# One wait per batch instead of two before the row gathers of a two-layer graph attention kernel

## The chip, the cores and the metric

The kernel runs on one core of one Trainium2 chip. A core has five engines that run side by side: TensorE (PE: matmuls, with its weight loads shown as PEld), VectorE (DVE), ScalarE (ACT), GpSimd (POOL) and SyncE (SP), and 16 DMA engines that move data. The engines have queues of their own and meet only at semaphores: an instruction counts a semaphore up when it is done, and another engine waits until the count is high enough. The metric is the device time of one execution in microseconds (us). The time before is 1787.6 us, the median of three executions (1787.34, 1787.60 and 1789.18 us).

## The reference

Two layers of graph attention over 3125 nodes with 128 features and 53125 directed edges, sorted by their destination. For each edge the keys and values of its source node are needed; softmax runs over the edges of one destination. Cut to what matters here:

```python
# layer 0 (x is normalised first); layer 1 adds an edge term to k and v
q, k, v = h @ Wq + bq, h @ Wk + bk, h @ Wv + bv
e = sum(q[d_all] * k[s_all], axis=-1) / sqrt(16)      # 8 heads of 16
p = exp(e - segment_max(e, d_all)[d_all])
alpha = p / segment_sum(p, d_all)[d_all]
agg = segment_sum(alpha[:, :, None] * v[s_all], d_all)
x = residual + agg.reshape(n, 128) @ Wo + bo
x = x + gelu(layer_norm(x) @ W1 + bf1) @ W2 + bf2
# layer 1: k_j = k[src] + edge_attr @ We, v_j = v[src] + edge_attr @ We, then the same
```

## The kernel before

**Tiles.** The edges are padded to 53248 and cut into 26 batches (`G`) of 16 tiles (`J`) of 128 edges, one edge to a partition. Each layer first computes the keys and values of all nodes and stores them in a table in HBM (`kv_table`, 256 floats a node). Then it goes once through the 26 batches. After that come the output projection, the normalisation and the feed-forward part, blocks of 128 nodes at a time.

**A batch.** GpSimd fetches the rows of its 2048 source nodes with 16 indirect DMAs (L464), one for each tile of 128 edges, into one of four slots of the tile `KV` (`SLOTS` = 4, slot = n % 4). The first eight count the semaphore `gathered[s][0]` up, the last eight `gathered[s][1]`. VectorE waits for the one before it works on the tiles of the first half (`add_edges`, L996), and for the other before those of the second half. TensorE makes each edge's query row from one-hot matrices (L732, L733), VectorE multiplies it with the keys (L1008) and adds up the heads (L1015), and the softmax of the batch before runs in between. VectorE then weighs the values in place in `KV` (`weigh`, L1120), and TensorE adds them up by destination in four quarters of four tiles (`add_up`, L778). Each quarter counts `agg_ready` up by one, so a batch adds 4. After the second quarter the first half of the slot is free, after the fourth the whole slot.

**What sets the order around the change.** Each engine's program is written out in Python, in rounds: in round n VectorE does the logits of batch n and the softmax of n - 1, TensorE adds up batch n - 2, and GpSimd runs freely ahead as far as the four slots allow. GpSimd has nothing else to do during the batches. Its `gather(n)` waits for the list of indices (`idx_loaded`), and before each half for `agg_ready` of batch n - 4: for the count after its second quarter before the first eight gathers, for the count after its fourth before the last eight. `pool.sem_inc(S["pool_go"], 1)` is an instruction for that wait to sit on; nobody reads the semaphore. SyncE loads the indices of batch n + 4 when the second half of batch n has landed (`indices`, L299).

Of the kernel before, what the change touches and what calls it, by code (L numbers as in the profile page):

```python
# [26 lines left out]
J = 16  # L27
G = 26
# [9 lines left out]
SLOTS = 4  # L38
# [3 lines left out]
def build(nc, a, out):  # L42
# [4 lines left out]
    kv_table = nc.dram_tensor("kv_table", (NP, 2 * D), F32, kind="Internal").ap()  # L47
# [6 lines left out]
    with ExitStack() as ctx:  # L54
# [3 lines left out]
        def sem(name):  # L58
# [6 lines left out]
        KV = sb("KV", [P, SLOTS, J, 2 * D])  # L65
# [11 lines left out]
        idx = sb("idx", [P, SLOTS, J], U32)  # L77
# [95 lines left out]
        S = {n: sem(n) for n in """x_loaded x2_loaded dst_loaded dste_loaded gates_in first_weights weights_loaded  # L173
            rel_stored block_loaded gate_stored edges_stored edges_loaded
            rel_loaded gate_loaded windows_stored last_loaded out_stored""".split()}
# [47 lines left out]
        def done(name, n):  # L223


            return S[name], n + START
# [18 lines left out]
        gathered = [[sem(f"gathered{s}{hh}") for hh in range(2)] for s in range(SLOTS)]  # L245
# [151 lines left out]
        @block.gpsimd  # L397
        def _(pool):
            g = nc.gpsimd
            g.memset(We[:, :], 0.0).then_inc(S["we_zeroed"], 1)  # L400
            g.memset(ones[:, :], 1.0).then_inc(S["consts_made"], 1)
            g.memset(ones3[:, :], 1.0).then_inc(S["consts_made"], 1)
            g.memset(one_col[:, :], 1.0).then_inc(S["consts_made"], 1)
            g.memset(ident[:, :], 0.0).then_inc(S["consts_made"], 1)
            g.memset(hsel[:, :], 1.0).then_inc(S["consts_made"], 1)
            g.memset(max_row[:, :], 0.0).then_inc(S["consts_made"], 1)
            g.memset(sum_rows[:, :], 0.0).then_inc(S["consts_made"], 1)
            g.memset(SUG[:, :], 0.0).then_inc(S["consts_made"], 1)
            g.memset(QT[:, NP:NP + P], 0.0).then_inc(S["consts_made"], 1)
            g.memset(minus_big[:, :], -BIG).then_inc(S["consts_made"], 1)  # L410
            pool.wait_ge(*done("consts_made", 10))
            g.affine_select(out=ident[:, :], in_=ident[:, :], compare_op=ALU.not_equal, fill=1.0,
                            base=0, pattern=[[-1, P]], channel_multiplier=1).then_inc(S["consts_made"], 1)
            by_head = hsel[:, :].rearrange("p (h c) -> p h c", h=H)
            g.affine_select(out=by_head, in_=by_head, compare_op=ALU.is_ge, fill=0.0,
                            base=0, pattern=[[-C, H], [0, C]], channel_multiplier=1).then_inc(S["consts_made"], 1)
            g.iota(iota_row[:, :], pattern=[[1, P]], base=0, channel_multiplier=0,
                   allow_small_or_imprecise_dtypes=True).then_inc(S["consts_made"], 1)
            g.iota(minus_part[:, :], pattern=[[-P, 2]], base=0, channel_multiplier=-1,
                   allow_small_or_imprecise_dtypes=True).then_inc(S["consts_made"], 1)  # L420
            g.iota(iota_part[:, :], pattern=[[P, 2]], base=0, channel_multiplier=1,
                   allow_small_or_imprecise_dtypes=True).then_inc(S["consts_made"], 1)
            pool.wait_ge(*done("consts_made", 12))
            g.affine_select(out=by_head, in_=by_head, compare_op=ALU.is_ge, fill=0.0,
                            base=C - 1, pattern=[[C, H], [0, C]], channel_multiplier=-1).then_inc(S["consts_made"], 1)

            g.memset(own_tiles, 1.0).then_inc(S["gates_made"], 1)
            g.memset(SAME[:, CH:CH + 4], 0).then_inc(S["gates_made"], 1)
            by_tile = own_tiles.rearrange("p (q k) -> p q k", k=TK)
            pool.wait_ge(*done("gates_made", 1))  # L430
            g.affine_select(out=by_tile, in_=by_tile, compare_op=ALU.is_equal, fill=0.0,
                            base=0, pattern=[[-1, TP], [0, TK]], channel_multiplier=1).then_inc(S["gates_made"], 1)
            g.memset(AGG[:, :], 0.0).then_inc(S["gates_made"], 1)

            pool.wait_ge(S["weights_loaded"], 16 * WEIGHTS)
            g.tensor_tensor(FB[:, 1, :], FB[:, 1, :], GB[:, 1, :], ALU.add).then_inc(S["fb_made"], 1)
            for l in range(2):
                if l:

                    def keep(n, k):  # L440
                        pool.wait_ge(*done("xn_ready", n + (2 * NB + 1)))
                        pool.sem_inc(S["pool_go"], 1)
                        g.tensor_copy(X[:, ds(n * P, P)], xn[k]).then_inc(S["x_kept"], 1)

                    def shift(n, k):
                        pool.wait_ge(*done("batch_step", n + 1))
                        pool.sem_inc(S["pool_go"], 1)
                        g.tensor_tensor(X[:, ds(n * P, P)], X[:, ds(n * P, P)], GB[:, 3, :], ALU.add).then_inc(S["x_shifted"], 1)

                    pipelined(pool, (keep, 4), (shift, 0))  # L450

                for k in range(4):
                    pool.wait_ge(kv_stored[k], 16 * kv_uses[k] * (l + 1))

                def gather(n):
                    s, u = n % SLOTS, n // SLOTS + 1 + uses[n % SLOTS] * l
                    pool.wait_ge(idx_loaded[s], u * 16)
                    if l == 0 and n == 2:
                        pool.wait_ge(S["edges_stored"], 64)
                    for hh in range(2):  # L460
                        pool.wait_ge(*done("agg_ready", n * 4 + (4 * G * l + 2 * hh + 2 - 4 * SLOTS)))
                        pool.sem_inc(S["pool_go"], 1)
                        for j in range(hh * 8, hh * 8 + 8):
                            g.indirect_dma_start(KV[:, s, j, :], None, kv_table,  # L464
                                                 bass.IndirectOffsetOnAxis(ap=idx[:, s, j:j + 1], axis=0)).then_inc(gathered[s][hh], 16)

                for n in range(G):
                    gather(n)

                if l == 0:  # L470

                    for b, w in quads:
                        at = slice(b * P, (b + w) * P)
                        pool.wait_ge(*done("res_ready", b + w))
                        pool.sem_inc(S["pool_go"], 1)
                        g.tensor_tensor(X[:, at], X[:, at], Y[:, at], ALU.add).then_inc(S["x_pair"], w)
                        pool.wait_ge(*done("x_pair", b + w))
                        pool.sem_inc(S["pool_go"], 1)
                        x3 = X[:, at].rearrange("p (b d) -> p b d", b=w)
                        g.tensor_tensor(x3, x3, FB[:, 0, :].unsqueeze(1).broadcast_to([P, w, D]), ALU.add).then_inc(S["x_summed"], w)  # L480
                else:
                    pool.wait_ge(*done("fb_made", 1))

                    def affine(n, k):
                        at = ds(n * P, P)
                        pool.wait_ge(*done("xn_ready", n + (3 * NB + 1)))
                        pool.sem_inc(S["pool_go"], 1)
                        g.tensor_tensor(Y[:, at], Y[:, at], GB[:, 0, :], ALU.mult).then_inc(S["ln_affine"], 1)
                        pool.wait_ge(*done("ln_affine", n * 3 + 1))
                        pool.wait_ge(*done("tp_ready", n + (3 * NB - 1)))  # L490
                        pool.sem_inc(S["pool_go"], 1)
                        g.tensor_tensor(hN[k], Y[:, at], GB[:, 1, :], ALU.add).then_inc(S["ln_affine"], 1)
                        pool.wait_ge(*done("ln_affine", n * 3 + 2))
                        pool.sem_inc(S["pool_go"], 1)
                        g.tensor_tensor(Y[:, at], Y[:, at], FB[:, 1, :], ALU.add).then_inc(S["ln_affine"], 1)

                    blocks(pool, affine)


                    def scale_last(n, k):  # L500
                        pool.wait_ge(*done("xn_ready", n + (4 * NB + 1)))
                        pool.wait_ge(*done("x_out", n - 1))
                        g.tensor_tensor(hN[k], xn[k], GB[:, 2, :], ALU.mult).then_inc(S["ln_last"], 1)

                    blocks(pool, scale_last)
# [871 lines left out]
```

## Time and profile before

| | us |
|---|---|
| median of three executions | 1787.6 |
| lowest and highest | 1787.34, 1789.18 |
| profiled execution, from its first to its last instruction (the span) | 1423.2 |
| what the median has beyond that span | 364.4 |
| GpSimd busy in the span | 901.0 (63%), of it the 832 gathers 810.3 |
| VectorE busy | 1076.5 (76%) |
| TensorE busy | 1072.8 (75%) |
| ScalarE busy | 840.3 (59%) |

The profile gives no time of the profiled execution other than its span, so the span is set beside the median of the executions that were timed. The 364.4 us between them lie before the first and after the last instruction that the trace holds, or in the way in which the two are taken; no view divides them. Times inside the span are read as microseconds from its start. "Idle before" is the time in which an engine stood before an instruction, and the name behind it is the work whose end released it; "issue" means that the engine waited for nothing that the profile shows. Register and semaphore instructions are not counted as busy, and no view has rows of their own for them.

### The profile page before, as it was taken

The numbers are of one execution on the slowest core, as the hardware profiler recorded it, in microseconds if no ns is written. First come the engines' busy times: TensorE is split into PE (matmuls) and PEld (weight loads), VectorE is DVE, ScalarE is ACT, GpSimd is POOL, SyncE is SP. The second block draws the span as 40 slices with busy tenths as digits, with TensorE's granted clock in tenths as the row PEclk, the third lists the DMA queues.
The fourth block names the chain that finished last, engine by engine and source line by source line (L and its number), as shares of the span: only waits on it lengthen the run. The fifth ranks groups of instructions, "written<-read, shape, count | busy, mean of one in ns | idle before, by whom it ended". The sixth has DMA issues, their size and how long they took to land. (4 is left out here: it accounts for less than half of the span.)

```text
span 1423.2 us, 28503 instructions
## 1 busy us (share of the span) xinstructions
PE 1072.8 (75%) x6809; PEld 956.7 (67%) x6809; DVE 1076.5 (76%) x2695; ACT 840.3 (59%) x2605; POOL 901.0 (63%) x1028
## 2 busy tenths in 40 slices
PE   3937678767877787768896788888888888887790
PEld 1436677667866776758735677787787778776690
DVE  5538877787877787865443888988988898897557
ACT  1615776676667666644443467766776676576351
POOL 2177777777777777531046777777777777770453
PEclk9967877787777777778897989999999999898795
DMA  5385555555555565420024567667766766671001
GB/s 157 106 182 178 173 188 194 191 155 189 193 186 159 192 193 171 137 91 0 7 79 141 176 211 223 197 193 220 214 199 196 224 207 189 219 229 48 1 1 45
DMA packets 100659, 222.50 MB, mean 156 GB/s; under 512 B 34875, under 2 KB 49882, under 8 KB 96941
## 3 DMA queue, kind: packets, MB, share of 16 engines
q0 software_dynamic: 39936, 109.11, 26.8%
q1 hardware_dynamic: 57927, 109.78, 22.8%
q10 hardware_dynamic: 2662, 2.05, 0.5%
q8 instruction: 56, 0.92, 0.3%
q14 instruction: 78, 0.64, 0.1%
HBM read 184.86 MB, written 36.00 MB: 155 GB/s over the span
## 5 line engine op out<-in xcount | busy, mean ns | idle before, releaser
L464 POOL DMA_INDIRECT KV<-kv_table,idx x832 | 810.3, 974 | 301.5 <-issue 247.4
L732 PE MATMUL PS<-QT,OHT 128*128 x1664 | 401.6, 330 | 146.5 <-DVE OHT L990 122.3
L732 PEld LDWEIGHTS PS<-QT,OHT 128*128 128x128 f32 x1664 | 317.9, 236 | 166.1 <-issue 164.6
L733 PE MATMUL PS<-QT,OHT 128*128 x1664 | 390.4, 324 | 0.0
L733 PEld LDWEIGHTS PS<-QT,OHT 128*128 128x128 f32 x1664 | 319.1, 238 | 0.0
L592 ACT ACTIVATE AGG<-AGG,PC,RCS x800 | 309.3, 387 | 3.1 <-ACT AGG L588 2.4
L1008 DVE TENSOR_TENSOR PR<-KV,PS 128x512 f32<-128x512 f32 x208 | 140.6, 676 | 105.6 <-DMA KV<-kv_table,idx 103.7
L778 PE MATMUL PS<-OH,KV 128*128 128x128 f32 x1600 | 208.4, 280 | 2.9 <-DVE OH L1110 1.2
L588 ACT ACTIVATE AGG<-PS 128x127 f32 x800 | 208.0, 260 | 1.0 <-issue 0.7
L778 PEld LDWEIGHTS PS<-OH,KV 128*128 128x128 f32 x1600 | 196.7, 197 | 5.6 <-issue 2.6
L584 ACT ACTIVATE PC<-PS 128x4 f32<-128x4 f32 x200 | 33.5, 168 | 267.1 <-PE PS L778 256.0
L1001 DVE TENSOR_TENSOR KV<-KV,PS 128x1024 f32<-128x1024 f32 x104 | 125.3, 1205 | 76.0 <-PE PS L743 47.5
L1015 DVE TENSOR_REDUCE Ls<-PR 128x32 f32<-128x512 f32 x208 | 139.7, 672 | 0.2
L1120 DVE TENSOR_TENSOR KV<-KV,PS 128x512 f32<-128x512 f32 x208 | 128.6, 680 | 0.4 <-PE PS L753 0.3
L568 ACT ACTIVATE OHT<-REL,minus_part 128x1024 f32<-128x1024 bf16 x104 | 113.0, 1134 | 19.9 <-PE PS L733 19.9
L743 PE MATMUL PS<-We,EA 128*128 128x256 f32 x416 | 118.3, 424 | 0.0
L571 ACT ACTIVATE OHT<-OHT,one_col 128x1024 f32<-128x1024 f32 x104 | 112.9, 1133 | 0.0
L753 PE MATMUL PS<-ident,AL 128*128 128x128 f32 x52 | 21.1, 405 | 105.9 <-DVE AL L1095 105.9
L743 PEld LDWEIGHTS PS<-We,EA 128*128 128x128 f32 x416 | 86.9, 226 | 10.6
L753 PEld LDWEIGHTS PS<-ident,AL 128*128 128x128 f32 x52 | 8.4, 161 | 118.5 <-DVE AL L1095 118.5
L660 ACT ACTIVATE KV<-PS,bf 128x128 f32<-128x128 f32 x208 | 59.4, 368 | 44.5 <-PE PS L854 37.3
L990 DVE TENSOR_SCALAR OHT<-REL,iota_part 128x1024 f32<-128x1024 bf16 x104 | 79.5, 766 | 0.0
(158 smaller groups left out, 1352.2 us busy)
## 6 DMA issues: line engine op xcount, KB each, us to landing
REL<-rel_dram SPq DMA_DIRECT2D x52, 512.0 KB, 4.4
window_dram<-OH SPq DMA_DIRECT2D x25, 1024.0 KB
OH<-window_dram SPq DMA_DIRECT2D x50, 512.0 KB, 6.1
KV<-kv_table,idx POOLq DMA_INDIRECT x832
EA<-in_edge_batch SPq DMA_DIRECT2D x52, 256.0 KB
kv_table<-KV SPq DMA_DIRECT2D x52, 128.0 KB, 1.7
X<-in_x SPq DMA_DIRECT2D x2, 832.0 KB, 10.1
GATES<-edge_gates SPq DMA_DIRECT2D x8, 208.0 KB, 10.0
```

The source lines that it names most:

```text
L464: g.indirect_dma_start(KV[:, s, j, :], None, kv_table, bass.IndirectOffsetOnAxis(ap=idx[:, s, j:j + 1], axis=0)).then_inc(gathered[s][hh], 16)
L568: sc.activation(OHT[:, 1, nf, :], REL[:, 8 * P:16 * P], ACT.Abs, bias=minus_part[:, nf:nf + 1]).then_inc(S["oht2_step"], 1)
L588: sc.activation(AGG[:, ds(at + 1, P - 1)], bank[:, m, 1:P], ACT.Copy).then_inc(S["act_col"], 1)
L592: sc.activation(AGG[:, ds(at, 1)], AGG[:, ds(at, 1)], ACT.Identity, bias=PC[:, m:m + 1], scale=RCS[:, n % SLOTS, j:j + 1]).then_inc(S["act ...
L732: te.matmul(o, OHT[:, q // 2, 0, e0:e0 + P], QT[:, ds(blk, P)], start=True, stop=False)
L733: last = te.matmul(o, OHT[:, q // 2, 1, e0:e0 + P], QT[:, ds(blk + P, P)], start=False, stop=True)
L743: last = te.matmul(PS[2 + q % 2][:, 2 * m * D:2 * (m + 1) * D], EA[:, e0:e0 + P], We[:, :], start=True, stop=True)
L778: last = te.matmul(PS[4 + q % 2][:, m * P:(m + 1) * P], KV[:, n % SLOTS, j, D:2 * D], at[:, j * P:(j + 1) * P], start=True, stop=True)
L1001: v.tensor_tensor(kv, kv, ep, ALU.add).then_inc(S["e_used"], 1)
L1008: v.tensor_tensor(PR[:, q % 2, :].rearrange("p (j d) -> p j d", j=4), KV[:, n % SLOTS, 4 * q:4 * q + 4, 0:D], PS[q % 2][:, :].rearrange("p ...
L1015: v.tensor_reduce(Ls[:, :].rearrange("p (h j) -> p j h", h=H)[:, 4 * q:4 * q + 4, :], PR[:, q % 2, :].rearrange("p (j h c) -> p j h c", j= ...
L1120: v.tensor_tensor(v4, v4, at, ALU.mult).then_inc(S["pv_ready"], 1)
```

## The change

In `gather(n)` the loop over the two halves is gone. GpSimd waits once per batch, for the count of `agg_ready` that stood before the second half, and then issues all 16 gathers. The semaphore that each gather counts up is the same as before.

```diff
-                    for hh in range(2):
-                        pool.wait_ge(*done("agg_ready", n * 4 + (4 * G * l + 2 * hh + 2 - 4 * SLOTS)))
-                        pool.sem_inc(S["pool_go"], 1)
-                        for j in range(hh * 8, hh * 8 + 8):
-                            g.indirect_dma_start(KV[:, s, j, :], None, kv_table,
-                                                 bass.IndirectOffsetOnAxis(ap=idx[:, s, j:j + 1], axis=0)).then_inc(gathered[s][hh], 16)
+                    pool.wait_ge(*done("agg_ready", n * 4 + (4 * G * l + 4 - 4 * SLOTS)))
+                    pool.sem_inc(S["pool_go"], 1)
+                    for j in range(J):
+                        g.indirect_dma_start(KV[:, s, j, :], None, kv_table,
+                                             bass.IndirectOffsetOnAxis(ap=idx[:, s, j:j + 1], axis=0)).then_inc(gathered[s][j // 8], 16)
```

GpSimd's queue at batches 4 and 5 of the first layer, before the change. A row is one instruction or a run of like ones; `idx_loaded0` is the list of indices of slot 0, `agg_ready` the count of added-up quarters.

```order
L464 DMA KV<-kv_table,idx 128x256 [waits idx_loaded0,agg_ready]
L464 DMA KV<-kv_table,idx 128x256 x7
L464 DMA KV<-kv_table,idx 128x256 [waits agg_ready]
L464 DMA KV<-kv_table,idx 128x256 x7
L464 DMA KV<-kv_table,idx 128x256 [waits idx_loaded1,agg_ready]
L464 DMA KV<-kv_table,idx 128x256 x7
L464 DMA KV<-kv_table,idx 128x256 [waits agg_ready]
```

The same place of GpSimd's queue after the change, with the first gather of batch 6 as its last row.

```order
L463 DMA KV<-kv_table,idx 128x256 [waits idx_loaded0,agg_ready]
L463 DMA KV<-kv_table,idx 128x256 x15
L463 DMA KV<-kv_table,idx 128x256 [waits idx_loaded1,agg_ready]
L463 DMA KV<-kv_table,idx 128x256 x15
L463 DMA KV<-kv_table,idx 128x256 [waits idx_loaded2,agg_ready]
```

The wait between the eighth and the ninth gather is gone from each of the 52 batches; its count is now waited for eight gathers earlier. No gather has changed its place.

GpSimd's queue at the end of the first layer's batches before the change; `res_ready` counts blocks of the output projection.

```order
L464 DMA KV<-kv_table,idx 128x256 [waits idx_loaded1,agg_ready]
L464 DMA KV<-kv_table,idx 128x256 x7
L464 DMA KV<-kv_table,idx 128x256 [waits agg_ready]
L464 DMA KV<-kv_table,idx 128x256 x7
L476 TENSOR_TENSOR X<-X,Y 128x512 [waits res_ready]
L480 TENSOR_TENSOR X<-X,FB 128x512 [waits x_pair]
```

The same place after the change, from the last gathers of batch 24 on.

```order
L463 DMA KV<-kv_table,idx 128x256 x15
L463 DMA KV<-kv_table,idx 128x256 [waits idx_loaded1,agg_ready]
L463 DMA KV<-kv_table,idx 128x256 x15
L475 TENSOR_TENSOR X<-X,Y 128x512 [waits res_ready]
L479 TENSOR_TENSOR X<-X,FB 128x512 [waits x_pair]
```

What follows the gathers stands where it stood. The instructions of the other four engines are the same in the same order.

## Rows read from the trace of the kernel before

**Rows 1.** Busy time by stage: layer 0 from 66 us, layer 1 from 752 us.
```profile
core 0: us, PE busy (x) PEld busy (x) DVE busy (x) ACT busy (x) POOL busy (x), PEclk, DMA share, GB/s
66.00:597.00 531.00, 392.03 (x2526) 374.07 (x2525) 406.17 (x977) 342.11 (x1055) 404.17 (x416) 0.76 0.59 181
...
752.00:1285.00 533.00, 432.20 (x2883) 397.40 (x2882) 452.26 (x978) 336.54 (x1033) 406.01 (x416) 0.90 0.66 203
```

**Rows 2.** Waits of layer 0's steady part, 147 to 597 us: total, times, longest.
```profile
POOL KV L464 <- issue: 102.4, 336, 0.3
...
DVE PR L1008 <- DMA KV<-kv_table,idx: 82.0, 22, 4.9
...
POOL KV L464 <- PE PS L778: 5.2, 17, 0.3
```

**Rows 3.** Waits of layer 1's steady part, 833 to 1284 us.
```profile
POOL KV L464 <- issue: 107.2, 352, 0.3
...
DVE KV L1001 <- PE PS L743: 44.6, 22, 3.1
...
DVE KV L1001 <- DMA KV<-kv_table,idx: 1.3, 1, 1.3
```

**Rows 4.** All gathers: duration in ns, lowest, median and highest.
```profile
L464 POOL DMA_INDIRECT KV<-kv_table,idx x832: 942/946/1472, 65.9 to 1283.6; - x167
```

**Rows 5.** Timeline, GpSimd, batch 4 of layer 0: start, duration; eighth and ninth gather, first of batch 5.
```profile
147.55 0.95 POOL L464 DMA_INDIRECT KV<-kv_table,idx  x1 [0.31 <-issue]
...
156.47 0.95 POOL L464 DMA_INDIRECT KV<-kv_table,idx  x1 [0.30 <-issue]
157.73 0.95 POOL L464 DMA_INDIRECT KV<-kv_table,idx  x1 [0.30 <-issue]
...
167.80 0.94 POOL L464 DMA_INDIRECT KV<-kv_table,idx  x1 [0.30 <-issue]
```

**Rows 6.** Timeline, TensorE: adding up batch 0 of layer 0, the first slot given back.
```profile
120.17 2.86 PE L778 MATMUL PS<-OH,KV 128*128 128x128 f32 x16
124.65 1.06 PE L778 MATMUL PS<-OH,KV 128*128 128x128 f32 x8
127.33 1.06 PE L778 MATMUL PS<-OH,KV 128*128 128x128 f32 x8
```

**Rows 7.** Timeline, TensorE and GpSimd: batch 9 added up, batch 13's first gather, layer 0.
```profile
302.75 2.06 PE L778 MATMUL PS<-OH,KV 128*128 128x128 f32 x16
306.78 1.06 PE L778 MATMUL PS<-OH,KV 128*128 128x128 f32 x8
309.46 1.06 PE L778 MATMUL PS<-OH,KV 128*128 128x128 f32 x8
...
330.77 0.95 POOL L464 DMA_INDIRECT KV<-kv_table,idx  x1 [0.30 <-issue]
```

**Rows 8.** Timeline, TensorE and GpSimd, layer 1: batch 21 added up, batch 25's first gather.
```profile
1242.47 1.95 PE L778 MATMUL PS<-OH,KV 128*128 128x128 f32 x16
1246.04 1.06 PE L778 MATMUL PS<-OH,KV 128*128 128x128 f32 x8
1249.59 1.06 PE L778 MATMUL PS<-OH,KV 128*128 128x128 f32 x8
...
1264.33 0.95 POOL L464 DMA_INDIRECT KV<-kv_table,idx  x1 [0.30 <-issue]
```

**Rows 9.** Timeline, layer 1: batch 14 added up, batch 18's first gather.
```profile
1103.66 1.06 PE L778 MATMUL PS<-OH,KV 128*128 128x128 f32 x8
...
1120.61 0.95 POOL L464 DMA_INDIRECT KV<-kv_table,idx  x1 [0.30 <-issue]
```

**Rows 10.** Timeline, layer 0: fifth gather of a half (its first at 299.87).
```profile
299.87 0.95 POOL L464 DMA_INDIRECT KV<-kv_table,idx  x1 [0.30 <-issue]
...
304.87 0.96 POOL L464 DMA_INDIRECT KV<-kv_table,idx  x1 [0.30 <-PE PS L778]
```

**Rows 11.** Timeline, GpSimd: the first gather of layer 1.
```profile
752.10 0.99 POOL L464 DMA_INDIRECT KV<-kv_table,idx  x1 [2.18 <-DMA kv_table<-KV]
```

## The prediction

> **What bounds the kernel now.** I read the busy time by stage first, then the waits of each stage, then GpSimd's timeline at the places where the two waits stand. The stages [rows 1] show that the gathers fill both passes over the batches: 416 of them in the 531 us of layer 0 and 416 in the 533 us of layer 1, together 1064 of the span's 1423.2 us. The change touches nothing outside these. The waits of the steady part of layer 0 [rows 2] show who is last there: VectorE stands 22 times for the gathered rows, 82.0 us in all, 3.7 us per batch, while GpSimd never stands longer than 0.3 us. So GpSimd's pace is the pace of layer 0. One gather has a median of 946 ns [rows 4] and 0.30 us of idle time before it, 1.25 us together; 16 of them make 20.0 us, and the batch of [rows 5] takes 167.80 - 147.55 = 20.25 us. In layer 1 it is different [rows 3]: from 833 us on VectorE stands once, 1.3 us, for gathered rows, and 22 times, 44.6 us in all, for TensorE's edge matmuls. The loop between VectorE and TensorE sets the pace there. GpSimd still shows no idle time but the 0.3 us before each gather, so it is not held by a free slot either; it simply keeps up.
>
> What matters for this change is the row that should show GpSimd waiting for a free slot. It is there, "POOL KV L464 <- PE PS L778", 5.2 us in 17 times, longest 0.3 us [rows 2]. That is 0.3 us each, exactly what every gather has before it with no wait at all. It is the ordinary gap with another name on it, and in layer 1's steady part the row is missing.
>
> **What the change removes.** Per batch it takes one wait and the instruction that carries it out of GpSimd's queue, 52 in all. Their cost can be read at the ninth gather of a batch, before which the wait stood: 156.47 to 157.73 is 1.26 us from start to start, with 0.30 us idle [rows 5], and a gather without a wait has the same 0.30 us. The rows are rounded to 0.01 us, so one removed wait gives back at most about 0.01 us, 52 of them 0.5 us. The outer bound is that the whole gap of 0.30 us went with the wait: 26 x 0.30 = 7.8 us in layer 0, where GpSimd sets the pace, and nothing in layer 1. I take 0, because the gap before a gather with a wait is that of one without. What hides the wait is the gather that runs while the wait is being worked off.
>
> **What the change adds or moves.** The wait for the whole slot now stands before the first gather of a batch, where a wait for half of it stood. Behind it are queued all 16 gathers of the batch, and for them wait VectorE (both halves) and SyncE, which loads the next indices after the second half. The question is when the whole slot is free, against when the first gather of the batch starts.
> - Layer 0, first reuse of a slot: batch 0 is added up by 127.33 + 1.06 = 128.39 us [rows 6], and batch 4 starts its gathers at 147.55 us [rows 5]. The margin is 19.2 us. With the old wait (first half free at 120.17 + 2.86 = 123.03 us) it was 24.5 us.
> - Layer 0, steady: batch 9 is done at 309.46 + 1.06 = 310.52 us, batch 13 starts at 330.77 us [rows 7], margin 20.3 us. The old one was 330.77 - 304.81 = 26.0 us.
> - Layer 1, steady: batch 14 is done at 1103.66 + 1.06 = 1104.72 us, batch 18 starts at 1120.61 us [rows 9], margin 15.9 us.
> - Layer 1, last batch: batch 21 is done at 1249.59 + 1.06 = 1250.65 us, batch 25 starts at 1264.33 us [rows 8]. The margin is 13.7 us, the smallest of the 44 batches that reuse a slot.
>
> A margin of the gather's start is not yet one of the wait, because GpSimd's sequencer, which works off the waits, reads ahead of the engine. The trace shows it: the gather at 304.87 us is the fifth of its half and has no wait of its own, yet the trace names the adding up as what released it [rows 10]. So a wait for that count was worked off there, and the nearest half that has one begins at least four gathers, 5 us, later. I can't read the full distance from a view. It doesn't decide: while the sequencer stands at a wait, the gathers that it has already handed over go on running. What must fit between the freeing of the slot and the start of the first gather is only the handing over. The nearest row for that is the first gather of layer 1, which starts 2.18 us after its last release, with an empty queue [rows 11]. 2.2 us against 13.7 us: no gather starts later. The cost lies between 0 and 0; were the cover gone, it would be that of the slow rival below. Nothing else moves: the 832 gathers, the semaphores that they count up and every other engine's program are as they were.
>
> Here the Trainium skill speaks against the change ("Advanced Engine Details and Errata", Sequencer and Instruction Queues, Engine Queue Depths): it gives GpSimd a queue 8 instructions deep. By it the sequencer would meet the new wait about 8 x 1.25 = 10 us (an estimate with that page's depth) before the gather starts, and the margin at the wait itself would shrink from 13.7 to 3.7 us in the last batch. It would still pass without standing, so the sum stays. That [rows 10] show a wait worked off in mid-half agrees with such a queue; its depth no row here shows.
>
> **The sum.** Layer 0: 0 for the removed waits, 0 for the moved one. Layer 1: 0 and 0. The span stays at 1423.2 us, and as the 364.4 us between span and median are not touched, the median stays at 1787.6 us.
>
> **The rivals.**
> - *The removed waits were paid for (faster).* If the 0.30 us before the ninth gather fell away, layer 0 would lose 7.8 us: 1779.8 us. For it speaks that VectorE really waits for these gathers, so each 0.01 us counts 26 times. Against it speaks the equal gap with and without a wait. The Trainium skill puts 50 to 100 ns on reading a semaphore from a sequencer ("Advanced Engine Details and Errata", Miscellaneous Facts, Network/Comms). By that page the removed waits would be worth up to 26 x 0.1 = 2.6 us in layer 0 (an estimate), 1785.0 us, if they weren't hidden; the rows show no such difference. Chance of this rival: 0.04.
> - *The wait for the whole slot decides (slower).* Then gathering batch n hangs on the last quarter of batch n - 4 rather than on its second. That would lengthen a loop of four batches by the time between these quarters: 128.39 - 123.03 = 5.4 us in layer 0, 1250.65 - 1244.42 = 6.2 us in layer 1. 22 batches per layer reuse a slot, which is 5.5 rounds of four: 5.5 x 5.4 + 5.5 x 6.2 = 64 us, 1851 us. It would decide from the point at which the margin falls under the 2.2 us of handing over, that is if slots came free 11.5 us later than now in layer 1's last batch, or 14 to 18 us later in the others. For it speaks only that the margin in layer 1 is the smaller one. If it held in the last batch alone, it could not cost more than 6.2 us. Chance: 0.03.
> - *The gathers meet VectorE's instructions at another phase.* A gather's duration goes up to 1472 ns against a median of 946 [rows 4]. In layer 0 this adds 404.17 - 416 x 0.946 = 10.6 us [rows 1]. Should the removed instructions shift the gathers by a few hundredths of a microsecond, that sum could become anything from nothing to double: 1777 to 1798.2 us. Against it speaks that the starts don't move, by the above. Chance: 0.03, either way.
>
> **How the numbers follow.** Forecast 0.90, faster rival 0.04, slower rival 0.03, phase 0.03. What the measurement can tell from no change is about 0.2%, 3.6 us. The forecast lies within it, the first two rivals on their own side, the third is split. That gives faster 0.05, same 0.91, slower 0.04. The executions of before spread over 1.8 us (1787.34 to 1789.18), so the range of the forecast is the median with a little more than that on either side, 1785.4 to 1790.0 us. It takes in the skill's 2.6 us nearly whole and the 0.5 us of the rounding. The three rivals, together 0.10, are left out.
>
> **What would show it right or wrong.** In the profile after, the gathers of a batch should still take 20.2 to 20.5 us and have 0.30 us idle before each, the ninth too. If the ninth shows less, the faster rival is right. The first gather of a batch should start within some tenths of a microsecond of where it did, 13 us or more after the last quarter of the slot. If idle time over 0.3 us appears before it with L778 behind it, the slower rival is right, and then VectorE's wait for gathered rows, 3.7 us per batch in layer 0, must have grown too. The total of the gathers' durations should stay near 810 us. If it is off by more than 3 us, the phase has shifted. The prediction is wrong if the median leaves 1785.4 to 1790.0 us.

## The result and the profile after

The kernel with one wait per batch takes 2070.25 us (2062.1 to 2075.23, four runs), the kernel before in the same comparison 1788.39 us (1787.34 to 1796.03). The ratio is 1.1557, 95% interval 1.1517 to 1.1597: 282 us, 15.6%, slower. The forecast was 1787.6 us. The numbers below can't be understood without one thing: these kernels have two kinds of execution, both seen on one and the same chip at different times, one in which before takes some 1427 us and one in which it takes some 1788 us, so each time is given with that of before beside it.

The profile after is of an execution of 2067.39 us with a span of 2065.4 us. Two rows of its page, GpSimd's gathers and the largest wait of ScalarE (line numbers from L464 on are one less than before), and under them the same two rows of the page before:
```profile
L463 POOL DMA_INDIRECT KV<-kv_table,idx x832 | 793.1, 953 | 909.2 <-issue 859.0
L583 ACT ACTIVATE PC<-PS 128x4 f32<-128x4 f32 x200 | 34.1, 170 | 811.1 <-remote 715.1
...
L464 POOL DMA_INDIRECT KV<-kv_table,idx x832 | 810.3, 974 | 301.5 <-issue 247.4
L584 ACT ACTIVATE PC<-PS 128x4 f32<-128x4 f32 x200 | 33.5, 168 | 267.1 <-PE PS L778 256.0
```
The waits of the whole execution after (engine, line, what ended the wait: us in total, times, longest):
```profile
POOL KV L463 <- issue: 859.0, 830, 47.4
ACT PC L583 <- remote: 715.1, 46, 17.3
DVE KV L1000 <- remote: 394.2, 24, 44.4
PE PS L731 <- DVE PR L1007: 324.0, 30, 36.0
```
The engines' own work is nearly what it was: the gathers take 793.1 us, against 810.3 before. What grew is above all idle time; TensorE's busy time grew too, from 1072.8 to 1142.9 us, at a lower granted clock (last section). GpSimd stood no longer than 0.3 us in the steady parts of before [rows 2, 3]; now its idle time before gathers is 909.2 us in the whole execution, against 301.5 before, and up to 47.4 us at once. In before's rows VectorE waits for gathered rows or TensorE's edge matmuls, a few us at a time; now it waits 24 times, 394.2 us, for something that the profile calls "remote", a release that it can't assign.

Where GpSimd stands is seen in the timeline. Batch 0's last adding-up and batch 4's first gather, layer 0, then batch 1's last quarter and batch 5's first two gathers, and in layer 1 a batch's last quarter and a first gather:
```profile
181.92 1.06 PE L777 MATMUL PS<-OH,KV 128*128 128x128 f32 x8
183.78 0.94 POOL L463 DMA_INDIRECT KV<-kv_table,idx  x1 [35.50 <-issue]
...
214.26 1.06 PE L777 MATMUL PS<-OH,KV 128*128 128x128 f32 x8
216.11 0.94 POOL L463 DMA_INDIRECT KV<-kv_table,idx  x1 [12.21 <-issue]
217.36 0.95 POOL L463 DMA_INDIRECT KV<-kv_table,idx  x1 [0.30 <-issue]
...
1606.92 1.06 PE L777 MATMUL PS<-OH,KV 128*128 128x128 f32 x8
1608.78 0.94 POOL L463 DMA_INDIRECT KV<-kv_table,idx  x1 [14.45 <-issue]
```
In each case the first gather follows the last quarter of its slot by 0.8 us (216.11 - 215.32, 183.78 - 182.98, 1608.78 - 1607.98). The trace shows the same 0.8 us at all 44 batches that reuse a slot. So the wait for the whole slot decides at every one of them, where in [rows 5 to 9] it had 13.7 to 20.3 us to spare. Within a batch the ninth gather still has 0.30 us before it. From batch 5 to batch 25 one batch takes 30.9 us in layer 0 and 34.2 us in layer 1, against 20.4 and 20.5 us in the profile of before.

### The profile page after: what moved, and what is told of

It reads as the page before. It is cut to its first block and busy times, and to the rows that moved or that the text cites. A ratio compares the mean times of both kernels' runs of the same rounds, so it can differ in the third digit from the quotient of the medians.

```text
span 2065.4 us, 28451 instructions
## 1 busy us (share of the span) xinstructions
PE 1142.9 (55%) x6809; PEld 1017.7 (49%) x6809; DVE 1078.9 (52%) x2695; ACT 842.9 (41%) x2605; POOL 884.1 (43%) x1028
## 3 DMA queue, kind: packets, MB, share of 16 engines
q0 software_dynamic: 39936, 109.11, 18.4%
## 5 line engine op out<-in xcount | busy, mean ns | idle before, releaser
L463 POOL DMA_INDIRECT KV<-kv_table,idx x832 | 793.1, 953 | 909.2 <-issue 859.0
L731 PE MATMUL PS<-QT,OHT 128*128 x1664 | 426.1, 346 | 512.1 <-DVE PR L1007 324.0
L731 PEld LDWEIGHTS PS<-QT,OHT 128*128 128x128 f32 x1664 | 343.6, 253 | 541.8 <-issue 538.4
L732 PE MATMUL PS<-QT,OHT 128*128 x1664 | 409.5, 336 | 17.4 <-issue 17.2
L583 ACT ACTIVATE PC<-PS 128x4 f32<-128x4 f32 x200 | 34.1, 170 | 811.1 <-remote 715.1
L1000 DVE TENSOR_TENSOR KV<-KV,PS 128x1024 f32<-128x1024 f32 x104 | 125.8, 1209 | 436.8 <-remote 394.2
L732 PEld LDWEIGHTS PS<-QT,OHT 128*128 128x128 f32 x1664 | 339.9, 253 | 19.0 <-issue 19.0
L777 PE MATMUL PS<-OH,KV 128*128 128x128 f32 x1600 | 248.0, 307 | 166.8 <-ACT AGG L591 136.1
L777 PEld LDWEIGHTS PS<-OH,KV 128*128 128x128 f32 x1600 | 227.6, 220 | 169.9 <-issue 166.4
L587 ACT ACTIVATE AGG<-PS 128x127 f32 x800 | 208.4, 260 | 0.8 <-issue 0.4
L742 PE MATMUL PS<-We,EA 128*128 128x256 f32 x416 | 106.4, 390 | 0.0
L872 DVE TENSOR_TENSOR_SCAN FW<-GA,PS 128x128 f32<-128x128 bf16 x52 | 21.7, 417 | 120.8 <-issue 104.9
L742 PEld LDWEIGHTS PS<-We,EA 128*128 128x128 f32 x416 | 76.3, 199 | 7.6
```

The costliest lines, as they stand in the source:

```text
L463: g.indirect_dma_start(KV[:, s, j, :], None, kv_table, bass.IndirectOffsetOnAxis(ap=idx[:, s, j:j + 1], axis=0)).then_inc(gathered[s][j // ...
L587: sc.activation(AGG[:, ds(at + 1, P - 1)], bank[:, m, 1:P], ACT.Copy).then_inc(S["act_col"], 1)
L731: te.matmul(o, OHT[:, q // 2, 0, e0:e0 + P], QT[:, ds(blk, P)], start=True, stop=False)
L732: last = te.matmul(o, OHT[:, q // 2, 1, e0:e0 + P], QT[:, ds(blk + P, P)], start=False, stop=True)
L742: last = te.matmul(PS[2 + q % 2][:, 2 * m * D:2 * (m + 1) * D], EA[:, e0:e0 + P], We[:, :], start=True, stop=True)
L777: last = te.matmul(PS[4 + q % 2][:, m * P:(m + 1) * P], KV[:, n % SLOTS, j, D:2 * D], at[:, j * P:(j + 1) * P], start=True, stop=True)
```

## Experiments

**The kernel before, the value, and the number of waits.** Three kernels, run once each; before beside them took 1429.0 us. control changes nothing. two_full keeps two waits, both for the whole slot:
```
-pool.wait_ge(*done("agg_ready", n * 4 + (4 * G * l + 2 * hh + 2 - 4 * SLOTS)))
+pool.wait_ge(*done("agg_ready", n * 4 + (4 * G * l + 4 - 4 * SLOTS)))
```
quarters has four waits of four gathers each, each for its own quarter (`for q in range(4)`, `... + q + 1 - 4 * SLOTS`).

> The kernel before, unchanged, to see the profile of an execution that takes what the timed ones take (1788 us); the profile on which the prediction rested had a span of 1423.2 us. Theory A (the slot loop): the span is about 1786 us, 2 us under the time, and GpSimd stands for more than 0.3 us before the first or the ninth gather of a batch, behind TensorE's adding up. Rival (something outside the span): the span is 1423 us again and 364 us lie outside.

> Two waits per batch as before, but both for the whole slot (the count of the fourth quarter). Theory A (it is the value that is waited for, not the number of waits): the time of the changed kernel, 2062 to 2075 us. Rival B (the instruction between the halves matters by itself, as a pause of GpSimd's queue): the time of before, 1788 us.

> Four waits per batch, each for its own quarter of the slot, four gathers behind each. Theory A (slot loop): the first four gathers may start about 1 us earlier (TensorE adds up quarters 0 and 1 in one go) and the third four some 3 us earlier than before, over a loop of four batches: 44 x 0.25 to 44 x 1 us less than before, 1744 to 1777 us. Rival B (only the number of pauses counts): two pauses fewer cost 282 us, so two more should gain something of that order, 1500 to 1650 us. Rival C (no effect below a half): 1788 us.

Measured: 1425.71, 1426.05 and 1421.02 us. Nothing tells the three apart, and the unchanged kernel is 363 us under its time in the first comparison, so none of the three met the executions that their expectations were about. Span and time differ by 1.7 us (1424.0 and 1425.71 in control), not by 364.

**The kernel after once more.** whole is the changed kernel itself, three rounds on another chip.

> The changed kernel again, against the kernel before. In the three runs so far the kernel before took 1426 to 1429 us, not 1788, and two waits for the whole slot took 1426 us: the value that is waited for did not matter there. Theory A (the whole slot costs only in executions in which TensorE's semaphore updates come late, as the trace of the 2067 us execution shows them): where before takes 1425 to 1430 us, the changed kernel takes the same, 1421 to 1430 us. Rival (taking away the ninth gather's wait instruction is what costs, whatever the state): 1660 us or more against 1427, a ratio near 1.16.

Measured: 1427.63 us (ten runs) against 1427.19 us, ratio 1.0002, 95% interval 0.9972 to 1.0033. The same code that cost 282 us costs nothing here. Its waits from 147 to 597 us, and its first gather of batch 4:
```profile
POOL KV L463 <- issue: 107.0, 351, 0.3
...
DVE PR L1007 <- DMA KV<-kv_table,idx: 85.4, 22, 5.0
```
```profile
130.88 1.06 PE L777 MATMUL PS<-OH,KV 128*128 128x128 f32 x8
...
150.91 0.95 POOL L463 DMA_INDIRECT KV<-kv_table,idx  x1 [0.31 <-issue]
```
These answer to [rows 2, 5, 6] and are the picture that the prediction drew: 19.0 us between the last quarter (131.94) and the gather, 0.31 us idle, VectorE's 82.0 us for gathered rows now 85.4.

**Make the loop bind.** The loop of slots is the circle in which a slot is gathered into, worked on, added up and so freed for the batch four later. It binds when GpSimd has to stand until a slot is free. If this loop is what costs, it must cost in the 1427 us executions too once it has only three batches in it. half3, whole3 and quarters3 are before, after and quarters with every awaited value raised by 4, one batch:
```
-n * 4 + (4 * G * l + 2 * hh + 2 - 4 * SLOTS)
+n * 4 + (4 * G * l + 2 * hh + 2 - 4 * SLOTS + 4)
```

> The two waits of each batch ask for the halves of the batch three before instead of four before, a stricter condition, so that the loop of slots has three batches in it and has to bind if it can. Loop theory (the whole-slot wait costs only where the loop slot free, gather, add up is the limit): from the rows of before, the start of a batch's gathers to the end of its adding up is four batches of 20.5 us less the margin of 13.7 to 20.3 us, so 62 to 68 us, and a wait for half a slot is let go 5.4 to 6.2 us earlier: (56 to 63) / 3 = 18.8 to 21 us per batch, no more than 0.5 us over the 20.5 us of now, so 1425 to 1450 us. Rival (a wait costs by being there or by its place in GpSimd's queue, and not by the loop): 1427 us, as before.

> One wait per batch for the whole slot of the batch three before. Loop theory: 62 to 68 us plus 0.8 us of wake-up over three batches is 21 to 23 us per batch against 20.5, over 46 batches 25 to 115 us more than before, 1450 to 1540 us, and 5.4 to 6.2 us / 3 = 1.8 to 2.1 us per batch (some 80 to 95 us) above half3 where both bind. The idle time before each batch's first gather should be in the trace. Rival (not the loop): within 5 us of half3 and of before.

> Four waits per batch, each for its own quarter of the slot of the batch three before. Loop theory: a quarter is free still one adding-up step earlier than a half, so this is the quickest of the three, at or below half3, 1420 to 1435 us. If instead the number of waits costs, it is the slowest of the three.

Measured, with before at 1419.64 us: half3 1429.66, whole3 1544.55, quarters3 1427.5 us. GpSimd's waits for the gathers, half3 first:
```profile
POOL KV L464 <- issue: 252.8, 825, 1.8
```
```profile
POOL KV L463 <- issue: 380.3, 829, 5.4
```
And two batches of whole3, the last quarter of a slot and the first gather into it:
```profile
290.83 1.06 PE L777 MATMUL PS<-OH,KV 128*128 128x128 f32 x8
292.68 0.94 POOL L463 DMA_INDIRECT KV<-kv_table,idx  x1 [1.44 <-issue]
...
312.68 1.06 PE L777 MATMUL PS<-OH,KV 128*128 128x128 f32 x8
314.54 0.94 POOL L463 DMA_INDIRECT KV<-kv_table,idx  x1 [1.45 <-issue]
```
Again 0.8 us from the last quarter to the gather. A batch takes 23.2 us in layer 0 and 23.0 in layer 1, in half3 20.5 and 20.6. So with three batches in the loop, waiting for the whole slot costs 115 us more than waiting for halves. half3 itself doesn't bind. Within each layer the first and ninth gathers of its batches have their 0.3 us of idle time and no more, but for one with 1.8 us, though the semaphore events of GpSimd show its sequencer standing 8 to 11 us at the first wait of each batch from the fourth of a layer on. Its 10 us over before lie within the 22 us over which before spread in the comparison with whole (1418.75 to 1440.57). whole3 came out 5 us above the range of the loop theory (1450 to 1540), which took 21 to 23 us per batch, and its distance to half3, expected at 80 to 95 us, is 115; the ranking and the place of the idle time are as the theory had them. Number of waits: quarters3 has four and is no slower than half3 with two.

**In search of the 1788 us executions.** control, two_full and quarters again, on yet another chip, as control_b, two_full_b and quarters_b.

> The kernel before unchanged, once more and perhaps on another chip. Both theories: either 1420 to 1440 us as in the runs of this study so far, or, if the execution is of the kind that the first measurement timed, 1788 us. In that second case the loop theory expects idle time of several us before each batch's first and ninth gather, TensorE's semaphores reaching VectorE, ScalarE and SyncE some 10 us after the matmuls while gathers run, and about 27 us per batch.

> Two waits per batch, both for the whole slot. If 1427 us executions: 1420 to 1440 us for every theory. If 1788 us executions: the loop theory (what matters is the value waited for) expects 2060 to 2075 us as with one wait; the rival (what matters is one wait instead of two) expects 1788 us.

> Four waits per batch, each for its own quarter. If 1427 us executions: 1420 to 1435 us. If 1788 us executions: the loop theory expects less than 1788 us, since the first gathers of a batch go on a quarter earlier, 1640 to 1780 us; the rival (number of waits) expects 1788 us or more.

Measured, before 1427.15 us: 1427.57, 1429.29 and 1422.13 us. They decide nothing but show the first three to repeat within 3.3 us.

**More traffic.** traffic and traffic_whole are before and after with 104 copies of 512 KB that nothing in the loop waits for. They read 54.5 MB and write as much (104 x 512 KB); the expectation below has twice that.
```
+for k in range(2):
+    act.dma_start(extra_dram[ds(n * 2 + (2 * G * l + k), 1), :, :] ...,
+                  a["edge_batch"][ds(n, 1), :, :] ...).then_inc(extra_stored, 16)
```

> The kernel before, with two copies of 512 KB from DRAM to DRAM added per batch (104 in all, on ScalarE's DMA queue), which nothing in the loop waits for; they add 109 MB read and 109 MB written to the 222 MB that the kernel moves. Theory T (TensorE's semaphore updates come late because DMA traffic stands in their way): with this traffic they should come late here too, the period of a batch grow by several us and the time rise over 1500 us, with VectorE starting on TensorE's results several us after the matmuls end. Rival (the late updates have another cause): only the transfers themselves get slower, each wake-up from TensorE stays under 0.1 us, and the time is 1425 to 1480 us.

> The kernel after (one wait for the whole slot), with the same added copies. Theory T with the loop theory: 60 us or more above the run with two waits. Rival: if the added traffic lengthens a batch's way from its gathers to its adding up by under 13.7 us, the smallest margin in the rows of before, it equals the run with two waits to within 10 us.

This time before itself took 1785.25 us, on the chip that had given 1427.15 us a while earlier. traffic took 1798.81 and traffic_whole 2065.26 us. Against before the copies add 13.6 us; against after's 2062 to 2075 us they add nothing, though the HBM moves 160 GB/s over the span instead of 107. In after, which has no such copies, TensorE's results come late too, as shown below; whether the copies would make them late in the 1427 us kind, which is what the two expectations were about, was not measured. The two are worth more as traces: traffic is the first with two waits in an execution of the 1788 us kind. GpSimd's gathers and ScalarE's wait in traffic (L467 and L587 are L464 and L584 of before):
```profile
L467 POOL DMA_INDIRECT KV<-kv_table,idx x832 | 802.4, 964 | 632.5 <-issue 456.6
L587 ACT ACTIVATE PC<-PS 128x4 f32<-128x4 f32 x200 | 34.8, 174 | 497.1 <-PE PS L785 246.4
```
Idle time before the gathers is 632.5 us with two waits and 907.3 in traffic_whole, 275 us more; the times differ by 266.5 us. A batch takes 25.3 and 27.3 us in the two layers with two waits, 31.1 and 34.2 with one. With some 21 batches per layer between, 21 x (5.8 + 6.9) = 267 us. The loss of the change is thus the growth of the period from batch to batch, from the first reuse of a slot on.

**The value or the number, where it costs.** two_full and quarters a third time, as two_full_c and quarters_c.

> Two waits per batch, both for the whole slot, once more, in the hope of executions in which before takes 1785 to 1790 us. There: the loop theory (the value waited for costs) expects 2060 to 2075 us, the rival (one wait in place of two costs) expects 1785 to 1790 us. Where before takes 1427 us: 1420 to 1440 us for both.

> Four waits per batch, each for its own quarter of the slot. Where before takes 1785 to 1790 us, the loop theory expects less than that, 1640 to 1780 us, since a quarter is free one adding-up step before a half; the rival expects no gain. Where before takes 1427 us: 1420 to 1435 us.

Before took 1784.39 us this time, so these two decide. two_full_c took 2070.59 us: two waits for the whole slot cost 286 us, as much as one. It is the value waited for, not one wait in place of two. quarters_c took 1840.87 us, 56 us slower than before, where the loop theory expected a gain of at least 4. That was a miss. In its trace a batch takes 25.5 us in layer 0, much as with halves, but 29.2 us in layer 1 against 27.3 (halves as in traffic, the only trace of them in this kind).

**Why the loop is so long there.** The traces of these executions answer that in part: results of TensorE reach the engines that wait for them late. Three places, in the engines' order of time. First after, layer 0, TensorE's matmuls of two quarters, GpSimd's last gather of the batch, ScalarE's copy that waits for these matmuls:
```profile
191.15 2.01 PE L777 MATMUL PS<-OH,KV 128*128 128x128 f32 x16
202.69 1.21 POOL L463 DMA_INDIRECT KV<-kv_table,idx  x1 [0.30 <-issue]
206.74 0.17 ACT L583 ACTIVATE PC<-PS 128x4 f32<-128x4 f32 x1 [15.88 <-remote]
```
The matmuls are over at 193.16 us. ScalarE, idle since 190.86, goes on at 206.74, 13.6 us later and 2.8 us after GpSimd's last gather has ended. Layer 1 of after shows it for two engines at once:
```profile
1583.32 1.89 PE L742 MATMUL PS<-We,EA 128*128 128x256 f32 x8
1585.16 1.73 PE L777 MATMUL PS<-OH,KV 128*128 128x128 f32 x14
1588.19 0.27 PE L777 MATMUL PS<-OH,KV 128*128 128x128 f32 x1 [0.46 <-issue]
1593.38 0.95 POOL L463 DMA_INDIRECT KV<-kv_table,idx  x1 [0.30 <-issue]
1597.48 1.22 DVE L1000 TENSOR_TENSOR KV<-KV,PS 128x1024 f32<-128x1024 f32 x1 [14.81 <-remote]
1597.59 0.17 ACT L583 ACTIVATE PC<-PS 128x4 f32<-128x4 f32 x1 [17.02 <-remote]
```
TensorE has finished at 1585.21 (edges) and 1588.46 us (adding up), the gathers end at 1594.33, and only at 1597.5 do VectorE and ScalarE wake, 0.1 us apart, though they wait for different counters of TensorE. With two waits the same thing is shorter. traffic, layer 0, a quarter's matmuls, the last gather of a run, ScalarE, and the next half's first gather:
```profile
188.19 1.06 PE L785 MATMUL PS<-OH,KV 128*128 128x128 f32 x8
194.16 0.95 POOL L467 DMA_INDIRECT KV<-kv_table,idx  x1 [0.30 <-issue]
196.47 0.17 ACT L587 ACTIVATE PC<-PS 128x4 f32<-128x4 f32 x1 [5.02 <-remote]
197.24 0.95 POOL L467 DMA_INDIRECT KV<-kv_table,idx  x1 [2.13 <-remote]
```
Matmuls over at 189.25, gathers at 195.11, ScalarE wakes at 196.47. GpSimd itself stands at the wait for that same counter, and during this stand the count arrives. With two waits GpSimd stops after eight gathers, with the value of the whole slot only after sixteen. ScalarE's longest such wait is 17.3 us in after and 7.1 in traffic. All its waits for that matmul, in traffic and in whole, an execution of the other kind:
```profile
ACT PC L587 <- PE PS L785: 246.4, 60, 7.3
ACT PC L587 <- remote: 236.1, 41, 7.1
...
ACT PC L583 <- PE PS L777: 246.7, 54, 7.2
```
Some 250 us of waiting belong to the order of the work, in whole and in before. With two waits the idle time before this instruction is 497.1 us, with one 811.1 us. In whole no wait has the name "remote". And while no gathers run, TensorE's results arrive at once in after as well: ScalarE's copy for batch 0 starts at 176.75 us, inside the run of matmuls that begins at 174.83.

The semaphore events of the traces say the same for all the counts of the adding up that they hold, each laid beside the end of its matmul; a run is a stretch of gathers with no gap over 1 us. In whole all 197 counts come within 0.02 us. In after 91 of 207 come over 1 us late, up to 15.8 us. Of the 91 whose matmul ended during a run of gathers 90 are late, of the 116 others one; two_full_c has 93 of 93 and none of 115; traffic, with its shorter runs, parts them less sharply, 79 of 87 and 24 of 120. 87 of the 91 late ones in after arrive while GpSimd stands, mostly some 3.2 us behind the end of its run, four inside a run. The counts that ScalarE raises with its copies (L583; the trace holds 204 of 208) come within 0.01 us in after too. A run of gathers alone doesn't do it: in whole 416 gathers follow one another without a break in each layer, and none of the 177 counts whose matmul ended in such a run is late.

The traces of this kind also lack most of their own semaphore records. Of the 13312 counts with which the gathers report that they have landed, after's trace holds 1979 and traffic's 2797, whole's 13104 and before's 13093. Every execution of the experiments was recorded, since each has its span. So that the lateness comes with the recording is a rival that no run here tests.

The worst case is the start of a layer, where four slots are free and nothing stops GpSimd for 64 gathers. After, layer 0:
```profile
102.64 0.64 PE L732 MATMUL PS<-QT,OHT 128*128 x2
141.34 0.69 DVE L1007 TENSOR_TENSOR PR<-KV,PS 128x512 f32<-128x512 f32 x1 [41.38 <-issue]
...
147.33 0.95 POOL L463 DMA_INDIRECT KV<-kv_table,idx  x1 [0.30 <-issue]
```
VectorE stands 41.38 us, with the queries that it waits for done at 103.28 us and the gathers of batch 0, its own, issued by 88 us and landed by 98. This one ended before the run of gathers did, so the end of a run isn't the only way out.

**A pause put in on purpose.** pace8 has GpSimd wait for the landing of its own eight gathers behind each half batch, pace_first only in the first four batches of a layer:
```
+if n < SLOTS:                                   # pace_first only
+    pool.wait_ge(gathered[s][hh], u * 128)
```

> The kernel before unchanged. Where executions take 1785 us: 88 to 100 us between its first batches' L778 and what waits for them while GpSimd's first 64 gathers run unbroken, later ends of ScalarE's waits for L778 at most 9 us after the matmuls. Where they take 1427 us: as the first control.

> Before, with a wait of GpSimd for the landing of its own eight gathers behind each half batch, so that no run of gathers is longer than eight. Theory B (an unbroken run of gathers holds TensorE's updates back in the 1785 us executions): GpSimd's own pace sets the time in both kinds of execution: 16 gathers of 1.25 us and two pauses of 2.1 us or so are 24.3 us per batch, which is 1427 + 50 x 3.8 = 1600 to 1650 us, and nearly the same time where before takes 1785 us, since the 80 us of unbroken gathers at each layer's start are broken too; so faster than before there by 100 us or more. Rival (the lateness has to do with something else): 1600 to 1650 us where before takes 1427, and 1850 us or more where before takes 1785.

> Before, with the wait for its own landing behind the half batches of each layer's first four batches only, where no wait for a slot stops GpSimd. Theory B: where before takes 1785 us the 69 to 83 us for which VectorE and ScalarE stand still at each layer's start shrink to under 10 us each time, which gives back 80 to 130 us, 1655 to 1705 us; where before takes 1427 us it costs up to 16 pauses of 2.1 us, 1427 to 1460 us. Rival: 1785 us or a little more.

> The pauses in each layer's first four batches only. Where before takes 1785 us, theory B expects 1680 to 1750 us (the stand of VectorE and ScalarE at each layer's start shrinks from 69 to 83 us to the length of a run of eight gathers, less 50 us for the pauses themselves, as the run of the other kind measured them); the rival expects 1785 to 1840 us. Where before takes 1427 us: 1477 us again.

Before took 1424.73 us beside the first three and 1424.1 us beside the last, so none was of the kind that could answer the question. control_c took 1432.92, pace8 1721.88, pace_first 1476.9, pace_first_b 1472.02 us (ratio 1.0334, 1.0297 to 1.0371). What they measured is the price of such a pause where nothing is late. pace8, two pauses:
```profile
309.14 1.31 POOL L464 DMA_INDIRECT KV<-kv_table,idx  x1 [2.69 <-DMA KV<-kv_table,idx]
...
323.40 0.94 POOL L464 DMA_INDIRECT KV<-kv_table,idx  x1 [4.20 <-DMA KV<-kv_table,idx]
```
2.69 and 4.20 us, not the 2.1 us that I had reckoned with, and a batch of 26.6 us in layer 0, not 24.3. Both kernels lose, pace8 21% and pace_first 3.3%, and both came out above what was expected of them in this kind (1600 to 1650 and 1427 to 1460 us). No count of the adding up or of the queries is late in pace8, but neither is one in whole.

## Why the prediction was wrong

- **What failed first is the last step of the sum**: "as the 364.4 us between span and median are not touched, the median stays at 1787.6 us". There is no such stretch beside the span. In every run of both kinds time and span are 1.7 to 2.1 us apart (2067.39 and 2065.4; 1798.81 and 1797.1; 1425.71 and 1424.0). By that, the profile with a span of 1423.2 us was of an execution of about 1425 us, and the times shown were of executions that took some 362 us more inside the span. So the table's reading of the 364.4 us as time beyond the span is wrong as well. Every row that I read was true, and of the other kind of execution.
- **The removed waits, 0 us**: right as far as the runs go. two_full (two waits) and whole (one) are both level with before in the 1427 us executions, and two_full_c and after agree at 2070.6 and 2070.25 us in the others. The faster rival fell with them.
- **The moved wait, margins of 13.7 to 20.3 us against 2.2 us of handing over, "no gather starts later"**: right for the executions it was read from (whole: ratio 1.0002), wrong for those that were timed, and this is the term of the sum, put at 0, that measured 282 us. There the margin is gone; the first gather hangs on the last quarter, 0.8 us behind it (so the handing over takes 0.8 us, not 2.2). whole3 shows the same mechanism where it can be switched on, 125 us over before, and half3, where the wait for halves still has its margin, doesn't.
- **The slow rival** had the mechanism right and two sizes wrong: its chance, 0.03, and its price, "64 us, 1851 us". It priced a loop of four batches at the distance from the second to the last quarter, 5.4 and 6.2 us [rows 6, 8]. In after that distance is 215.32 - 193.16 = 22.2 us in layer 0 and 1607.98 - 1588.46 = 19.5 us in layer 1, since the adding up of the second half waits for ScalarE, and ScalarE for the late count. By the rival's own rule 5.5 x 22.2 + 5.5 x 19.5 = 229 us (an estimate), against the 282 measured. The rest stays without a term of its own.
- **GpSimd's queue.** The prediction took from [rows 10] that the sequencer reads ahead. The depth of eight instructions that it took beside this from the Trainium skill ("Advanced Engine Details and Errata", Engine Queue Depths) isn't what the trace shows: in whole the semaphore events of GpSimd put its waits, from the third batch of a layer on, 15.3 to 15.8 us, twelve gathers, ahead of the gather behind them. By that nothing would be left of a margin of 13.7 us at the wait itself. That this wouldn't matter, since the engine goes on with the gathers handed over, held: in half3 the sequencer stands 8 to 11 us at each batch's first wait, and but for one of 1.8 us no gather within a layer starts later for it.

Shown, then: in both kinds of execution the value waited for costs only where the loop of slots binds; the loop of four binds in the 1788 us executions and not in the others; and in the former the results of TensorE reach the other engines late while a run of gathers goes on, longer with sixteen gathers in a run than with eight. That the run of gathers is what holds the counts back is not shown. It rests on the order of the ends (2.8, 3.2 and 1.4 us behind a run) and on the 90 of 91 against one of 116, while the same runs of gathers hold nothing back in the 1427 us kind, so that something else must be there too. The pause that was to test it met only that kind. Open are also whether the recording has a part in it, what puts an execution into one kind or the other (the chips numbered 2 and 6 gave both), and why quarters loses 56 us in one of them.

## What to carry to other kernels

Before a row is read, lay the span of the profile beside the time that is to be forecast: if they are hundreds of microseconds apart, the profile isn't of what was timed, and no margin in it may be spent. A ring of buffers with slack to spare is an insurance against late signals, so a wait should ask for the smallest piece that the next transfer needs; the coarser one cost nothing in one kind of execution and 15.6% in the other. But finer isn't always better: quarters lost 56 us to halves in one run of the second kind. To see whether a wait would ever decide, take one buffer out of its ring by raising the awaited count and run it.

## What the runs showed of the hardware

- The same kernel took 1427 and 1785 us on one chip at different times, with the engines' work nearly unchanged: in after and whole, which are one kernel in the two kinds, VectorE is busy 1078.9 and 1077.3 us, GpSimd 884.1 and 904.0 us. In DMA too the gathers' packets take the same engine time, 18.4% of 2065.4 us and 26.4% of 1426.5 us, 380 and 377 us.
- TensorE's counts of the adding up came within 0.02 us of the end of the matmul in whole, and over 1 us late in 91 of 207 cases in after, 90 of them among the 91 whose matmul ended while GpSimd was in a run of gathers.
- The mean of TensorE's granted clock was 0.747 in after and 0.855 in whole. Its matmuls are busy 1142.9 and 1055.5 us, 87 us of a difference of 639 us in span, so the lower clock accounts for 87 us at most and not for the rest.
- 104 copies of 512 KB from DRAM to DRAM beside the gathers added 13.6 us to a kernel of 1785 us (1798.81) and nothing that can be told to one of 2070 (2065.26).
- A wait for the landing of the last eight gathers stopped GpSimd for 302.3 us in 95 cases in pace8, 3.2 us each, 5.3 at most; before a gather whose semaphore had long been there it stood 0.30 us, as before any other.
